# Quarter products summed in PSUM: three banks a pair, both pairs interleaved, three joins in place of seven

## What is computed

```python
weights = _rfs(input_weights, ab, AB, proj_matrix)
feats = _rfs(x, ab, AB, proj_matrix)          # exp(x @ (ab*proj).T - correction)
x = _layernorm(x + einsum('bsr,or->bso', feats, weights))
real = einsum('bti,io->bto', x, cos(theta + theta_noise))
imag = einsum('bti,io->bto', x, sin(phi + phi_noise))
x = _layernorm(x + sqrt(real * real + imag * imag))
```

## Time and profile before

| | |
|---|---|
| median of 3 runs | 697.18 us (696.45 to 697.43) |
| profiled execution | 696.72 us |
| its span, first to last instruction | 694.9 us |
| granted TensorE clock, mean | 0.997 |
| busy: PE, PEld | 683.1 us (98%), 563.6 us (81%) |
| busy: DVE, ACT, POOL | 598.7 us (86%), 461.4 us (66%), 202.3 us (29%) |

### The profile page before, as it was taken

How to read it: one execution, slowest core, us unless ns; L and a number is a source line. 1 busy time by engine, 2 the same in 40 slices (tenths; PEclk the granted TensorE clock), 3 DMA queues, 4 the chain that set the end, 5 groups by cost and what they waited for, 6 DMA issues and landing times.

```text
span 694.9 us, 10320 instructions
## 1 busy us (share of the span) xinstructions
PE 683.1 (98%) x3026; PEld 563.6 (81%) x3026; DVE 598.7 (86%) x969; ACT 461.4 (66%) x697; POOL 202.3 (29%) x257
## 2 busy tenths in 40 slices
PE   9999999999999999999999999999999999999994
PEld 7888888878888888888888888888888888888883
DVE  5889899888789888888898888989888899988787
ACT  6868998395666748566674866757485575846446
POOL 5672304105032140503214050321405033050414
PEclk9999999999999999999999999999999999999998
DMA  8861041471826547182654708255480835534011
GB/s 301 244 137 60 16 121 62 112 206 39 211 85 144 159 110 207 30 214 88 137 165 103 214 21 217 94 122 180 93 224 16 205 112 121 181 79 118 0 61 61
DMA packets 168837, 88.11 MB, mean 127 GB/s; under 512 B 112624, under 2 KB 139248, under 8 KB 168816
## 3 DMA queue, kind: packets, MB, share of 16 engines
q1 hardware_dynamic: 166944, 84.46, 44.8%
q0 software_dynamic: 1152, 2.10, 1.8%
q10 hardware_dynamic: 720, 1.31, 0.5%
HBM read 57.41 MB, written 30.44 MB: 126 GB/s over the span
## 4 chain that ended last, share of the span: by engine, by line
PE 92%; DVE 4%; DMA 1%; ACT 1%; issue 1%; SPq 0%; POOL 0%; POOLq 0%; ACTq 0%; DVEq 0%
PE token_ps L1010 8%; PE token_ps L1011 8%; PE token_ps L1009 8%; PE token_ps L1127 6%; PE token_ps L1129 6%; PE token_ps L1128 6%; PE project_ps L953 5%; PE project_ps L954 4%; PE project_ps L955 4%; PE project_ps L1127 4%; PE project_ps L1128 4%; PE project_ps L1129 4%; PE turn_ps L954 3%; PE turn_ps L955 3%; PE turn_ps L953 3%; PE turn_ps L1128 3%
## 5 line engine op out<-in xcount | busy, mean ns | idle before, releaser
L472 POOL TENSOR_TENSOR plain_late<-plain_late 128x1024 f32<-128x1024 f32 x26 | 67.6, 2599 | 262.4 <-ACT plain_late L848 262.4
L1009 PE MATMUL token_ps<-W_hi,F_hi 128*128 128x512 f32 x256 | 99.7, 389 | 0.0
L1011 PE MATMUL token_ps<-W_hi,F_lo 128*128 128x512 f32 x256 | 99.6, 389 | 0.0
L1010 PE MATMUL token_ps<-W_lo,F_hi 128*128 128x512 f32 x256 | 99.6, 389 | 0.0
L732 ACT ACTIVATE o_tile<-plain_late,shift,rstd 128x512 f32<-128x512 f32 x56 | 42.6, 808 | 60.2 <-POOL shift L489 56.0
L726 ACT ACTIVATE plain_late<-plain_late 128x1024 f32<-128x1024 f32 x28 | 29.7, 1062 | 75.1 <-POOL plain_late L472 73.7
L1127 PE MATMUL token_ps<-T_hi,zT_hi 128*128 128x512 f32 x170 | 66.4, 390 | 0.4 <-DVE zT_lo L1284 0.4
L1129 PE MATMUL token_ps<-T_hi,zT_lo 128*128 128x512 f32 x170 | 66.2, 389 | 0.0
L1128 PE MATMUL token_ps<-T_lo,zT_hi 128*128 128x512 f32 x170 | 66.1, 389 | 0.0
L618 ACT ACTIVATE F_hi<-plain_expo,ab 128x512 fp32r<-128x512 f32 x62 | 44.7, 721 | 32.2 <-DVE plain_expo L1289 32.1
L848 ACT ACTIVATE plain_late<-plain_late 128x1024 f32<-128x1024 f32 x54 | 55.3, 1056 | 14.6 <-DVE plain_late L1703 11.1
(11 more groups left out here) (285 smaller groups left out, 1789.7 us busy)
## 6 DMA issues: line engine op xcount, KB each, us to landing
x_tok<-in_x SPq DMA_DIRECT2D x16, 1024.0 KB, 6.1
out_tokens<-o_tile SPq DMA_DIRECT2D x62, 256.0 KB, 2.8
plain_xT_lo<-in_xT SPq DMA_DIRECT2D x14, 1024.0 KB, 9.0
turned_pair<-plain_late SPq DMA_DIRECT2D x104, 128.0 KB, 2.8
plain_zT_lo<-turned_pair SPq DMA_DIRECT2D x26, 256.0 KB, 2.8
plain_zT_lo<-turned_pair SPq DMA_DIRECT2D x52, 128.0 KB, 2.9
norm_bc<-token_norms SPq DMA_DIRECT2D x15, 256.0 KB, 3.1
z<-in_wT ACTq DMA_DIRECT2D x4, 256.0 KB, 4.7
```

The lines of the kernel that those rows point to most:

```text
L472: pool.tensor_tensor(parts[:, p, :, 0, :], parts[:, p, :, 0, :], parts[:, p, :, 1, :], ALU.add).then_inc(sum_made, 2)
L1009: nc.tensor.matmul(o, F_hi[:, c, cols], W_hi[:, c, :], start=(c == 0), stop=False)
L1010: nc.tensor.matmul(o, F_hi[:, c, cols], W_lo[:, c, :], start=False, stop=False)
L1011: return nc.tensor.matmul(o, F_lo[:, c, cols], W_hi[:, c, :], start=False, stop=(c == C - 1))
```

## The change

Each pair gets three banks in place of seven. Its bank for sums (`SUM_PS`) takes M1, and then M6, M5 and M3 are accumulated on top of it by PE (`opens=False`: no `start`), so that it holds in turn M1, U = M1 + M6, W = U + M5 and C12 = W + M3. Between two of them ACT copies the bank's contents out (`copy_first`, `copy_U`, `copy_W`), and the next product of that bank waits for the copy. `M7_PS` takes M7, and M4 on top of it after the join of C22; `M2_PS` takes M2. DVE is left with C11 = M1 + M2, C22 = W + M7 and C21 = U + (M7 + M4). The fourteen products of a step run in `PAIRED_ORDER`, both pairs interleaved. ACT squares C12 straight from PSUM and C11 by itself. `pair_sum` of pair 0 moves from POOL to the end of DVE's step, and tile 0's statistics from there to the start of the next step, behind the first residual; ACT's third and fourth `sum_square` move behind the first squares. The number of matmuls stays. Block 15 keeps its order of products and joins.

```diff
+        PAIRED_ORDER = [(0, "M1"), (0, "M7"), (0, "M2"), (0, "M6"), (1, "M1"), (0, "M5"), (1, "M7"),
+                        (1, "M6"), (0, "M3"), (1, "M5"), (0, "M4"), (1, "M3"), (1, "M2"), (1, "M4")]
+        PAIRED_JOINS = [(0, "C11"), (0, "C22"), (1, "C22"), (0, "C21"), (1, "C11"), (1, "C21")]
+        SUM_PS = [token_ps[0], project_ps[0]]
+        M7_PS = [token_ps[1], project_ps[1]]
+        M2_PS = [token_ps[2], turn_ps[0]]
...
@@ gpsimd, step
                 make_damp(b, mv_made)
-                pair_sum(b, 0)
                 pair_residual2(b, 0)
@@ scalar, step
+                def copy_U(p):
+                    act.wait_ge(quarter_done, paired_done(b, p, "M6"))
+                    nc.scalar.activation(parts[:, p, 1, 0, :], SUM_PS[p][:, :], ACT.Copy).then_inc(U_copied, 1)
+                def copy_W(p):
+                    act.wait_ge(quarter_done, paired_done(b, p, "M5"))
+                    nc.scalar.activation(parts[:, p, 1, 1, :], SUM_PS[p][:, :], ACT.Copy).then_inc(W_copied, 1)
...
                     features(C * (b + 2) + 3, 3, 1)
+                    copy_first(0)
                     round_halves(1)
                     round_half_sums(1)
-                    copy_first(0)
+                    copy_U(0)
                     load_table(ACT.Sqrt)
+                    copy_first(1)
+                    copy_W(0)
                     if ahead:
                         act.wait_ge(x_loaded[slot], 16 * (pair + 2))
-                        for j in range(C):
-                            sum_square(b + 3, j, slot, 1 - slot)
+                        sum_square(b + 3, 0, slot, 1 - slot)
+                        sum_square(b + 3, 1, slot, 1 - slot)
+                    copy_U(1)
+                    if ahead:
                         act.wait_ge(xT_loaded, 16 * (b + 2))
                         round_columns(0)
                         round_columns(1)
-                    copy_first(1)
-                    square_tile(0, 1)
-                    square_tile(0, 0)
+                    copy_W(1)
+                    square_C11(0)
+                    square_C12(0)
+                    if ahead:
+                        sum_square(b + 3, 2, slot, 1 - slot)
+                    square_second(0)
+                    if ahead:
+                        sum_square(b + 3, 3, slot, 1 - slot)
+                    square_C12(1)
                     pair_roots(b, 0)
-                    square_tile(1, 1)
-                    square_tile(1, 0)
+                    square_C11(1)
+                    square_second(1)
@@ tensor
+            def paired_products(b):
+                s = b - PLAIN
+                for p, name in PAIRED_ORDER:
+                    total, o7, o2 = SUM_PS[p][:, :], M7_PS[p][:, :], M2_PS[p][:, :]
                     if name == "M1":
                         pe.wait_ge(halves_lo_made, 2 * s + p + 1)
...
+                    if name == "M6":
+                        pe.wait_ge(first_copied, 2 * s + p + 1)
+                        quarter_product(total, half_sum(p, "S2"), quarter_sum("T2"), False)
                     if name == "M5":
+                        pe.wait_ge(U_copied, 2 * s + p + 1)
+                        quarter_product(total, half_sum(p, "S1"), quarter_sum("T1"), False)
+                    if name == "M3":
+                        pe.wait_ge(W_copied, 2 * s + p + 1)
+                        quarter_product(total, half_sum(p, "S4"), quarter(low_sin_hi, low_sin_lo, 0), False)
+                    if name == "M4":
+                        pe.wait_ge(joined, paired_joins_done(b, p, "C22"))
+                        quarter_product(o7, half(p, 2), quarter_sum("T4"), False)
@@ vector, step
-                    pair_stats2(b - 1, 0, 1)
-                    pair_stats2_made(b - 1, 0)
-                    residual1(b, slot, 0)
+                    residual1(b, slot, 0)
+                    pair_stats2(b - 1, 0, 0)
+                    pair_stats2(b - 1, 0, 1)
+                    pair_stats2_made(b - 1, 0)
+                    stats1(b, 0)
                     pair_moments2(0)
-                    stats1(b, 0)
...
                     split_feature_pair(C * (b + 2) + 3, 1)
-                    join_u(0)
...
-                    join_c12(0)
+                    paired_C11(0)
+                    paired_C22(0)
                     if ahead:
                         split_columns(b + 2, 0)
                         split_columns(b + 2, 1)
+                    paired_C22(1)
+                    paired_C21(0)
+                    pair_sum(b, 0)
+                    paired_C11(1)
+                    if ahead:
                         turn_norms(b + 3, 1 - slot)
-                    join_u(1)
...
-                    join_c12(1)
-                    pair_stats2(b, 0, 0)
+                    paired_C21(1)
```

More of the change, by code:

```diff
@@ L240, in build @@
         PLAIN = 2
-        QUARTER_ORDER = ["M1", "M6", "M7", "M5", "M2", "M4", "M3"]
         QUARTER_ORDER_LAST = ["M1", "M2", "M4", "M6", "M7", "M5", "M3"]
-        QUARTERS = len(QUARTER_ORDER)
-        JOIN_ORDER = ["U", "V", "C22", "W", "C11", "C21", "C12"]
+        QUARTERS = len(QUARTER_ORDER_LAST)
         JOIN_ORDER_LAST = ["U", "C11", "V", "C21", "C22", "W", "C12"]
-        JOINS = len(JOIN_ORDER)
+        JOINS_LAST = len(JOIN_ORDER_LAST)
         JOIN_CREDIT = 3
+        PAIRED_ORDER = [(0, "M1"), (0, "M7"), (0, "M2"), (0, "M6"), (1, "M1"), (0, "M5"), (1, "M7"),
+                        (1, "M6"), (0, "M3"), (1, "M5"), (0, "M4"), (1, "M3"), (1, "M2"), (1, "M4")]
+        PAIRED_JOINS = [(0, "C11"), (0, "C22"), (1, "C22"), (0, "C21"), (1, "C11"), (1, "C21")]
         MOVED = NB - 1 - PLAIN
@@ L252, in build, with paired_joins_done, last_joins_done, paired_done @@
         SUMS_ORDER = ["T1", "T3", "T2", "T4"]
-        def joins_done(b, p, order, *names):
-            return 2 * JOINS * (b - PLAIN) + JOINS * p + JOIN_CREDIT + max(order.index(name) for name in names) + 1
+        def paired_joins_done(b, p, name):
+            return len(PAIRED_JOINS) * (b - PLAIN) + JOIN_CREDIT + PAIRED_JOINS.index((p, name)) + 1
+        def last_joins_done(p, *names):
+            return (len(PAIRED_JOINS) * (NB - 1 - PLAIN) + JOINS_LAST * p + JOIN_CREDIT
+                    + max(JOIN_ORDER_LAST.index(name) for name in names) + 1)
+        def paired_done(b, p, name):
+            return len(PAIRED_ORDER) * (b - PLAIN) + PAIRED_ORDER.index((p, name)) + 1
+        def last_done(p, name):
+            return len(PAIRED_ORDER) * (NB - 1 - PLAIN) + QUARTERS * p + QUARTER_ORDER_LAST.index(name) + 1
+        PAIRED_SQUARES = [(0, "C11"), (0, "C12"), (0, "C21"), (0, "C22"), (1, "C12"), (1, "C11"), (1, "C21"), (1, "C22")]
+        def paired_square_done(b, p, name):
+            return 2 * C * b + SQUARE_CREDIT + PAIRED_SQUARES.index((p, name)) + 1
         NORMS_ON_PE = 2
@@ L1123, in quarter, with quarter_product @@
                 return [hi[:, at + i, :] for i in range(H)], [lo[:, at + i, :] for i in range(H)]
-            def quarter_product(o, left, right):
+            def quarter_product(o, left, right, opens=True):
                 for i in range(H):
-                    nc.tensor.matmul(o, left[0][i], right[0][i], start=(i == 0), stop=False)
-                    nc.tensor.matmul(o, left[0][i], right[1][i], start=False, stop=False)
-                    last = nc.tensor.matmul(o, left[1][i], right[0][i], start=False, stop=(i == H - 1))
+                    nc.tensor.matmul(o, left[0][i], right[0][i], start=(opens and i == 0), stop=False, skip_group_check=not opens)
+                    nc.tensor.matmul(o, left[0][i], right[1][i], start=False, stop=False, skip_group_check=not opens)
+                    last = nc.tensor.matmul(o, left[1][i], right[0][i], start=False, stop=(i == H - 1), skip_group_check=not opens)
                 last.then_inc(quarter_done, 1)
@@ L1147, in pair_products @@
                         else:
-                            pe.wait_ge(expo_made, C * (b + 2) + 4)
-                        quarter_product(o(name), half(p, 0), quarter(cos_hi, cos_lo, 0))
-                    if name == "M6":
+                            pe.wait_ge(expo_made, C * (b + 2) + 1)
+                        quarter_product(total, half(p, 0), quarter(cos_hi, cos_lo, 0), True)
+                    if name == "M7":
                         pe.wait_ge(half_sums_lo_made, 2 * s + p + 1)
@@ L1169, in pair_products @@
[L1169 to L1174, removed]
-                    if name == "M4":
[L1176 to L1186, removed]
+                            pe.wait_ge(expo_made, C * (b + 2) + 3)
+                        quarter_product(o2, half(p, 1), quarter(cos_hi, cos_lo, H), True)
@@ L1252, in step @@
                     pe.wait_ge(T_made, 4)
[L1253 to L1254 removed]
+                paired_products(b)
             def last_step(b):
@@ L1702, in join_c21 @@
                     joins(p, "V")
```

(6 more changed lines are left out.)

117 lines of the change are left out of this document (65 added, 52 removed).

## The result

The changed kernel takes 700.28 us in the median of five runs, the kernel before 696.62 in five: a ratio of 1.0047 with a 95% interval of 1.0029 to 1.0066, so slower by some 3.3 us. One of the five runs of the changed kernel, 765.93, is a slow one with a mean granted clock of 0.85 and is left out of the ratio; the other four have a median of 699.85. Run again later the kernel was at 699.78 against 696.69, 1.0044 (1.0028 to 1.0059). The prediction had said 697.9, 0.7 above before, with a range of 696.4 to 700.2; it had put 0.77 on no change. Of its own rivals, what came is A (the halves of pair 1 come too late), though in under half of the steps and not in all of them.

A forecast was written before the change was run, and what follows sets the result against it. PE was taken to bound the kernel. Stalls of 0.7 us, all other terms 0, gave 696.72 + 0.7 = 697.4 on the profiled execution, 697.18 + 0.7 = 697.9 on the median; 8-in-10 range 696.4 to 700.2.

The forecast's parts named there:

- Rival A: Pair 1's halves too late in every step, `split_halves(1)` over 5.3 us behind first product; 4.4 us slower, 701.6; chance 0.13.
- DVE's relief: In the loop, 47 us less DVE work over 13 steps lies beside PE, which waits for none: worth 0.
- The round trips through ACT: Six products a step wait for ACT's bank copies; all in time, the tightest by 0.5 us: worth 0.
- Rival B: A copy round trip through ACT misses its 0.5 slack in each step: 6.5 us slower, 703.7; chance 0.06.
- M1 of pair 1 as the place of loss: Pair 1's first product, now fifth, waits for `split_halves(1)` in steps 3 and 4: 0.7 us in all.
- The price of one stall: On PE, a stall costs 0.21 us beyond its lateness: 0.13 + 0.21 = 0.34 in each of two steps.
- DVE's list and the next step: DVE's list ends later, POOL's residual 1.1 us later, yet the next step's second residual is just in time: 0.
- the slack of 0.7: In step 8, `split_halves(1)` ends 4.71 us behind the first product; pair 1's first product is due at 5.44.
- The ends: In the last block, norms end about 1 us later on ACT; cost 0, or 0.2 us at worst.

The follow-up runs named there:

- e5: The kernel before with the fourteen joins of each step cut from 512 columns to 64: 696.55 us, ratio 1.0000.
- e1: The changed kernel with pair 0's second residual on VectorE at the end of its step, not on GpSimd: 697.91 us, ratio 1.0016.
- e7: e6 with bank waits of the last block moved from just ahead of its first quarter product to ahead of its fourth mix: 697.17 us, ratio 1.0005.
- e9: The changed kernel run again, unedited: 699.78 us, ratio 1.0044.
- e2: The changed kernel with pair 0's sum of squares back on GpSimd: 713.69 us, ratio 1.0245.
- e6: The changed kernel with pair 0's residual on VectorE, M1 of pair 1 as sixth product and ScalarE copies of M1 and U earlier: 697.36 us, ratio 1.0011.

## Why the prediction was right or wrong

**PE bounds the kernel, and DVE's relief is worth 0: right.** e5 shows it for DVE alone. The Trainium skill's rule ("Perfetto Trace Analysis", Identifying the Most-Contended Engine) judges PE's headroom by two measures, MFU and the weight loads' busy share. The prediction took the second alone, and by it DVE, at 87% against 83% for the weight loads, was the engine to relieve; e5 took it to 71% in the same stretch for no gain. So the measurement speaks against taking the weight loads' share by itself as the measure of PE's headroom in this kernel; MFU (the share of peak FLOP/s that the kernel's matmuls reach) wasn't worked out.

**The round trips through ACT fit by 0.5: right.** The copies stand where the list of due times had them (in step 8 `copy_U(0)` at 5.6 behind the first product, `copy_W(1)` at 13.8), and no loop step of the changed kernel waits for one. Rival B didn't come.

**M1 of pair 1 as the place of loss: right; its size: wrong.** The term was 0.7 us for two steps; it measured 2.4 in the profiled execution, with step 2. The new place alone is worth about what the term said: e1, which takes only the late start away, loses 0.8 in its loop, and its median is 1.25 above before, not 3.3. The rest, some 2 us, came with the step below. The price of one stall held. The remainder of step 3 on DVE, in the changed kernel's timeline:

```profile
189.74 0.96 DVE L1347 TENSOR_TENSOR zT_lo<-plain_zT_lo,zT_hi 128x768 fp32r<-128x768 f32 x1
```

It ended at 190.70, 0.28 behind M1's due time of 184.98 + 5.44 = 190.42, and the step lost 0.55; 0.28 + 0.21 makes 0.49.

**The step that failed is "DVE's list and the next step".** It had GpSimd's residual end 22.1 behind the first product of its step and called the list "just in time". In the changed kernel it ends at 369.51 + 2.41, 18.2 ahead of the next first product, which is 22.6 behind its own. Half a microsecond was lost in hand-overs that the sum had at nothing: in step 7 the pair's sum on DVE began 17.6 behind the first product and not 17.3, ACT's roots 18.9 and not 18.5, POOL's residual 20.15 and not 19.7. And the sum had the first residual out of the way before, an order that the kernel doesn't have. With 22.6 and the right order the same sum gives what was measured: 0.61 for the statistics, 0.59 for the residual, then the second statistics, `stats1` and the moments, and the second residual 15.47 ahead of the first product in place of 16.12. "Just in time" was 0.65 us late. The prediction had named what a miss would do ("move the transposes and, at the end, the halves, which have slack of their own"), but not put the two together: the slack of 0.7 that it read in step 8 was used up by the 0.65, with 2 us of scatter on top.

**The ends: wrong by a little.** The last block lost 0.37, where 0 or 0.2 at worst had been named. DVE's late list reached it: the second residual of block 15 started 0.20 later behind step 14's first product than before, the remainder that PE waits for 0.17 later. ACT went from the norms to the first turn without a wait, 0.16 later. The other 0.2 are the waits on banks long free, which the prediction didn't have (e7).

**Rival A** was the right mechanism with the right place. Its condition, `split_halves(1)` ending over 5.3 behind the first product, held in 5 of 13 steps of the profiled execution and in 6 of e9's. That its price, 4.4 for all 13 steps, is near the 3.3 measured is luck: most steps escape, while others are later than 0.13. Its chance of 0.13 was too low, since the case against it, step 8's slack, rested on a list in the wrong order.

**The range: luck too.** Its upper end, 700.2, is called half of A, but half of A's 4.4 would give 699.4, and no term gives 3.0 above before. The four runs' median of 699.85 lies inside it, the 700.28 of all five and the difference of 3.3 just outside.

## What to carry to other kernels

Where one engine is full and never waits, list what each of its instructions needs and when it is due; relief of another engine was worth nothing here (e5), and a product moved forward brings all the lateness of its operand's chain into the open. A slack smaller than the scatter of the DMAs in its chain is no slack: count how many steps would have missed it, not what one step shows. And an operation moved to a faster or slower engine has to be followed through to the next step's first wait: e1 and e2 move one operation of 1.2 or 2.4 us each, and lie 16 us apart.

## What the runs showed that I had not expected

GpSimd takes 2.4 us for an addition of 128x1024 where VectorE takes 1.2; at 24% busy it was on the path that decided the time. A satisfied wait was not free on TensorE when it was queued ahead of a product that stalls: 0.2 us for two of them in e6, gone in e7. And an execution of the changed kernel scatters more than one of the kernel before (698.0 to 702.0 against 696.0 to 698.0 in the same session), which fits a time that hangs on when DMAs land; e6, whose steps 3 to 14 hold no stall, is back to 696.9 to 697.9.
